# A message passing layer on one core: the edge stage with z in place in PSUM, and GpSimd left with the gathers

## The chip, the core and the metric

The kernel runs on one core of a Trainium2 chip. The core has TensorE (PE in the profile; its weight loads are PEld), VectorE (DVE), ScalarE (ACT), GpSimd (POOL) and SyncE (SP), and 16 DMA engines. The metric is device time in microseconds (us), from the kernel's start to its end; lower is better.

## The reference

One layer of a graph network over 1250 nodes and 20000 edges, in float32. The edges are sorted by their destination `dst`, and low node numbers have many more edges than high ones.

```
h      = relu(layernorm(x))                       # 1250 x 512
emb    = edge_attr @ W_edge + b_edge              # 20000 x 128 @ 128 x 512
msg    = relu(h[src] + emb)                       # 20000 x 512
aggr   = segment_sum(msg, dst, 1250)
h      = (1 + eps) * h + aggr
h      = gelu(layernorm(h @ W1 + b1))             # then W2, residual, layernorm
out    = x + layernorm(h + gelu(h @ M1) @ M2)
```

## The kernel before, in words

The kernel has three parts. First the node rows are normalized and written to DRAM as `gather_table` (with `b_edge` added), and DVE works out a plan from `dst`. Then comes the edge stage, of which this case is about. Last comes the node stage: W1, W2, M1 and M2, with layer norms between.

A **tile** is 128 edges, a **pair** two tiles, a **group** four tiles (`TPG`). There are 157 tiles with edges in 40 groups (`NG`); the last group has one such tile, and the kernel before computes two there. For each group:

- SP loads the transposed edge attributes into `attr_raw`. ACT rounds the first three tiles (`SPLIT`) to float32r, `attr_hi` (line 561). The rest, `attr_lo`, is subtracted by POOL for tiles 0 and 1 (line 455) and by DVE for tile 2 (line 922).
- PE multiplies by `W_edge` (`embed`). Tiles 0 to 2 take three float32r products each (lines 1100 to 1102), tile 3 one plain float32 product (line 1119), which the profile shows as two records. Pair 0 goes to `ps_u0` or `ps_t1` by turns, pair 1 to `ps_u1`.
- POOL gathers the source rows, one indirect DMA for a tile (line 472), by way of a small copy of the indices every two groups (`idx_now`, line 463). `rows` has two groups.
- DVE adds embedding and rows into `z` in SBUF (line 912, `z_done`). ACT writes `msg_hi`, relu of z rounded (line 660), and DVE writes `msg_lo`, the rest (line 916).
- ACT makes the 0/1 matrix `onehot` that says which node of a 128-node window each edge goes to: four squares into `apart` (line 594), then a relu (line 599).
- PE adds the messages into one PSUM half of `ps_t0` by `onehot` times `msg_lo` and `msg_hi` (line 1134, `scatter_last`).

Where the sorted edges pass from one window to the next inside a group (a **crossing**; there are nine), PE reads more of the plan into registers, adds the tiles of the old window with `onehot_first` (`scatter_extra`), and begins the new window with an identity product of the node rows (line 1127). ACT makes `onehot_first` (lines 606 and 613) and copies the old window out (line 624).

Each engine runs its own instructions in program order, and semaphores tie them together. There is no scheduler: the order is written out by hand in each engine's `group` or `step`. Most groups lie in loops whose body has four groups.

In the first four groups W1 is loaded, rounded by ACT (line 574) and its low part subtracted by DVE (line 939). The node stage does the same for later weights on POOL (line 504).

## Time and profile before

| | us |
|---|---|
| median of 3 runs (572.99 to 575.85) | 574.79 |
| the profiled execution, its own time | 573.92 |
| its span, first to last instruction | 572.0 |
| of it, first gather (27.4) to the last window copied out (311.7) | 284.3 |

Busy over the span: PE 468.2 (82%), DVE 410.2 (72%), POOL 337.1 (59%), ACT 307.4 (54%). The mean granted clock of TensorE is 0.966 of full speed. These shares mix the stages: in the edge stage the order of the engines is another, and a share says little there until the waits are read with it. "Idle before" is the time in which an engine did nothing ahead of an instruction, and the arrow names what ended it; "issue" means that the profile shows no wait.

### The profile page before, as it was taken

What the parts mean: (1) busy time and instruction counts of PE and PEld (TensorE: products, weight loads), DVE (VectorE), ACT (ScalarE), POOL (GpSimd) and SP (SyncE); (2) the same over time, 40 slices, a digit from 0 to 9 for tenths busy, and PEclk for the clock granted to TensorE, in tenths of its full rate; (3) what the DMA queues carried; (4) which work ended last, traced back from release to release, by engine and by line L of the source; (5) the groups of instructions that cost most, each with busy time, mean ns of one, the idle gap of its engine ahead of it and who ended that gap; (6) DMA issues with size and microseconds to landing.
All of it is one profiled execution on the core that took longest, in us unless ns stands there. A gap on an engine that the chain in (4) does not pass through costs nothing.

```text
span 572.0 us, 8417 instructions
## 1 busy us (share of the span) xinstructions
PE 468.2 (82%) x1959; PEld 356.2 (62%) x1960; DVE 410.2 (72%) x554; ACT 307.4 (54%) x569; POOL 337.1 (59%) x363
## 2 busy tenths in 40 slices
PE   1255887879777877889767999999999699999994
PEld 0133555656455554566545887778887489888883
DVE  7958869777767686779773577888999964473465
ACT  3848567676667685777872344446555556003100
POOL 4778878778787776778740244435777553150142
PEclk9999889899999999899997999999999799999998
DMA  8577666676666665676531922243441122021032
GB/s 279 215 243 246 207 202 205 187 204 184 199 194 196 197 202 167 187 211 206 166 111 42 328 75 73 92 146 112 147 147 56 55 74 74 19 93 37 5 106 73
DMA packets 34347, 85.27 MB, mean 149 GB/s; under 512 B 4928, under 2 KB 5264, under 8 KB 34320
## 3 DMA queue, kind: packets, MB, share of 16 engines
q0 software_dynamic: 12640, 41.43, 24.7%
q1 hardware_dynamic: 20864, 42.74, 22.4%
q10 hardware_dynamic: 816, 0.77, 0.5%
q8 instruction: 13, 0.21, 0.2%
q14 instruction: 14, 0.11, 0.1%
HBM read 72.34 MB, written 5.24 MB: 136 GB/s over the span
## 4 chain that ended last, share of the span: by engine, by line
PE 34%; issue 19%; DVE 18%; POOL 17%; DMA 6%; ACT 4%; POOLq 1%; DVEq 1%; another core or an unknown queue 0%; ACTq 0%; SPq 0%
POOL rows L472 11%; PE ps_t L1134 6%; DVE work L993 5%; PE ps_u L1100 5%; PE ps_u L1102 5%; PE ps_u L1101 5%; DMA rows<-gather_table,idx_now 4%; PE ps_t L1100 4%; PE ps_t L1101 4%; PE ps_t L1102 4%; DVE z L912 3%; POOL rstd L499 3%; POOL attr_lo L455 2%; ACT squares L716 2%; DVE lhs_lo L972 2%
## 5 line engine op out<-in xcount | busy, mean ns | idle before, releaser
L472 POOL DMA_INDIRECT rows<-gather_table,idx_now x158 | 173.1, 1095 | 57.4 <-issue 40.6
L912 DVE TENSOR_TENSOR z<-ps_u,rows 128x1024 f32<-128x1024 f32 x59 | 72.1, 1223 | 65.1 <-DMA rows<-gather_table,idx_now 32.7
L916 DVE SCALAR_TENSOR_TENSOR msg_lo<-z,msg_hi 128x1024 fp32r<-128x1024 f32 x79 | 96.2, 1258 | 0.0
L497 POOL TENSOR_TENSOR var_eps<-mv,eps_t 128x1 f32<-128x1 f32 x40 | 11.6, 290 | 143.3 <-ACT squares L716 77.1
L660 ACT ACTIVATE msg_hi<-z 128x1024 fp32r<-128x1024 f32 x79 | 82.4, 1043 | 2.3 <-DVE z L912 2.1
L1100 PE MATMUL ps_u<-we_hi,attr_lo 128*128 128x512 f32 x79 | 37.4, 474 | 45.6 <-POOL attr_lo L455 32.3
L1100 PE MATMUL ps_u<-w_hi,lhs_lo 128*128 128x512 f32 x160 | 64.7, 404 | 4.3 <-DVE lhs_lo L972 3.1
L1102 PE MATMUL ps_u<-w_hi,lhs_hi 128*128 128x512 f32 x160 | 62.9, 393 | 0.0
L1101 PE MATMUL ps_u<-w_lo,lhs_hi 128*128 128x512 f32 x160 | 62.8, 392 | 0.0
L1134 PE MATMUL ps_t<-msg_lo,onehot 128*128 128x512 f32 x146 | 62.1, 425 | 0.0
L1134 PE MATMUL ps_t<-msg_hi,onehot 128*128 128x512 f32 x146 | 60.4, 414 | 0.0
L1100 PEld LDWEIGHTS ps_u<-we_hi,attr_lo 128*128 128x128 f32 x79 | 15.8, 200 | 62.5 <-DVE z L912 19.6
L561 ACT ACTIVATE attr_hi<-attr_raw 128x384 fp32r<-128x384 f32 x40 | 20.6, 518 | 57.3 <-PE ps_u L1119 38.4
L594 ACT ACTIVATE apart<-iota,neg_rel_last 128x128 f32<-128x128 f32 x160 | 50.6, 387 | 0.0
L499 POOL TENSOR_TENSOR rstd<-var_eps,minus_half 128x1 f32<-128x1 f32 x40 | 40.3, 1007 | 3.1
L504 POOL TENSOR_TENSOR w_lo<-w_raw,w_hi 128x512 f32 (+1 forms) x24 | 35.0, 1462 | 9.4 <-ACT w_hi L711 9.4
L1119 PE MATMUL ps_u<-we_raw,attr_raw 128*128 128x512 f32 x78 | 40.5, 601 | 0.0
L1100 PE MATMUL ps_u<-ff_in_hi,w_lo 128*128 128x512 f32 (+1 forms) x96 | 34.8, 363 | 5.0 <-DVE ff_in_lo L968 5.0
L1100 PEld LDWEIGHTS ps_u<-w_hi,lhs_lo 128*128 128x128 f32 x160 | 30.1, 188 | 11.8 <-issue 3.3
L747 ACT ACTIVATE ff_full<-ps_u 128x512 f32<-128x512 f32 (+1 forms) x24 | 12.6, 527 | 43.4 <-PE ps_u L1102 39.5
L1134 PEld LDWEIGHTS ps_t<-msg_lo,onehot 128*128 128x128 f32 x146 | 30.2, 207 | 7.5 <-issue 0.5
L1101 PE MATMUL ps_u<-ff_in_lo,w_hi 128*128 128x512 f32 (+1 forms) x96 | 34.8, 362 | 0.0
(158 smaller groups left out, 1096.3 us busy)
## 6 DMA issues: line engine op xcount, KB each, us to landing
attr_raw<-in_attr_t SPq DMA_DIRECT2D x40, 256.0 KB
w_raw<-in_W SPq DMA_DIRECT2D x24, 256.0 KB, 2.7
tile_in<-mid SPq DMA_DIRECT2D x10, 512.0 KB, 3.2
res<-in_x SPq DMA_DIRECT2D x20, 256.0 KB, 2.6
xin<-in_x SPq DMA_DIRECT2D x5, 512.0 KB, 7.4
gather_table<-tab SPq DMA_DIRECT2D x5, 512.0 KB, 2.8
out<-work SPq DMA_DIRECT2D x10, 256.0 KB, 2.1
rows<-gather_table,idx_now POOLq DMA_INDIRECT x158
```

Source lines behind the costliest of these rows:

```text
L472: g.indirect_dma_start(rows[:, q, t, :], None, gather_table[:, :], bass.IndirectOffsetOnAxis(idx_now[:, slot, q * TPG + t:q * TPG + t + 1] ...
L499: g.tensor_tensor(rstd[:, slot:slot + 1], var_eps[:, slot:slot + 1], minus_half[:, 0:1], ALU.pow).then_inc(LN[ln]["rstd"], 1)
L504: g.tensor_tensor(w_lo[1 - s % 2][:, cols], w_raw[:, p, :], w_hi[1 - s % 2][:, cols].bitcast(f32), ALU.subtract).then_inc(w_lo_done, 1)
L594: last = a.activation(apart[:, e, :], iota[:, 0:P], ACT.Square, bias=neg_rel_last[:, ds(gr * TPG + e, 1)])
L660: a.activation(pair(msg_hi, r, p), pair(z, r % 2, p), ACT.Relu).then_inc(msg_hi_done, 1)
L912: v.tensor_tensor(pair(z, q, p), embedded(p, q)[:, :], rows[:, q, 2 * p:2 * p + 2, :].rearrange("p a d -> p (a d)"), ALU.add).then_inc(z_d ...
L916: v.scalar_tensor_tensor(pair(msg_lo, r, p), pair(z, r % 2, p), 0.0, pair(msg_hi, r, p).bitcast(f32), ALU.max, ALU.subtract).then_inc(msg_ ...
L1100: t.matmul(o, lhs[1][cols], rhs[0][rcols], start=first, stop=False)
L1101: t.matmul(o, lhs[0][cols], rhs[1][rcols], start=False, stop=False)
L1102: return t.matmul(o, lhs[0][cols], rhs[0][rcols], start=False, stop=last)
L1119: last = t.matmul(o, attr_raw[:, r, e * P:(e + 1) * P], we_raw[:, :], start=True, stop=True)
L1134: last = t.matmul(summed_in(bank), selection[:, e, :], m[:, r, e * D:(e + 1) * D], start=False, stop=(e == tiles[-1] and m is msg_hi), ski ...
```

## The change

- POOL only gathers in the edge stage, straight from `src_idx`; the 157 gathers are written out one after the other without a loop. `idx_now` and its copy are gone.
- `rows` has three groups instead of two. Each gather of a pair waits for the z of six pairs before (four before the change).
- z has no buffer of its own: DVE adds the rows in place in PSUM (`embedded`), over three pair buffers `ps_u0`, `ps_u1`, `ps_t1` in turn, and `msg_hi` and `msg_lo` read PSUM. PE may write a pair buffer again only when `msg_lo` of the pair three before is done; before, it waited for z.
- Two tiles of a group, the first of each pair, are split in three products, and the other two go through plain float32. DVE makes all of `attr_lo`. `attr_raw` has six slots, `msg_hi`, `msg_lo` and `onehot` have three groups.
- DVE's order alternates: add of a pair, then `msg_low` of the pair before it. ACT does `msg_hi` of pair 0 first, then `apart`, `msg_hi` of pair 1, `onehot`, and then the split of the group after next.
- PE scatters pair by pair, with an embedding ahead of each. The last group has one tile.
- W1 is loaded, rounded and split in the last groups. POOL makes its low parts after its last gather.
- Loop bodies have six groups; three groups stand ahead of the loop and seven behind.

```diff
-RING = 4
-HALF = EG // 2
-SPLIT = 3 * P
+RING = 3
+ATTRS = 6
+SPLIT = 2 * P
+HEAD, TAIL = 3, 7
...
-        attr_raw = sb("attr_raw", [P, RING, EG], f32, edge)
+        attr_raw = sb("attr_raw", [P, ATTRS, EG], f32, edge)
...
-        rows = sb("rows", [P, 2, TPG, D], f32, edge)
-        z = sb("z", [P, 2, 4 * D], f32, edge)
+        rows = sb("rows", [P, RING, TPG, D], f32, edge)
...
+        def embedded(g, p):
+            return (ps_u[0], ps_u[1], ps_t[1])[g.bank(p)][:, 0:D * g.in_pair(p)]
...
+            sp.wait_ge(emb_done[1], NG - TAIL + 1)
+            load_attr(NG - 1, (NG - 1) % ATTRS)
+            for c in range(W1_CHUNKS):
+                load_w1(c)
...
-            def two_groups(j, slot, split=True, pairs=2):
-                copy_idx(j, slot)
-                for q in range(2):
-                    gather(2 * j + q, q, 0, slot)
-                    if split:
-                        split_attr(2 * j + q, 2 * slot + q)
-                    if q == 0 or pairs == 2:
-                        gather(2 * j + q, q, 1, slot)
...
-            two_groups(0, 0, split=False)
-            with pool.Fori(0, NG // 4 - 1) as jj:
-                two_groups(2 * jj + 1, 1)
-                two_groups(2 * jj + 2, 0)
-            two_groups(NG // 2 - 1, 1, pairs=PAIRS)
+            for e in range(TILES):
+                group, pair_now = fixed(e // TPG), e % TPG // 2
+                if e % 2 == 0 and e // 2 >= 2 * RING:
+                    pool.wait_ge(z_done, e // 2 - 2 * RING + 1)
+                g.indirect_dma_start(rows[:, group.r, e % TPG, :], None, gather_table[:, :],
+                                     bass.IndirectOffsetOnAxis(src_idx[:, e:e + 1].bitcast(u32), 0)
+                                     ).then_inc(rows_in[group.slot(pair_now)], 16)
+            for c in range(W1_CHUNKS):
+                cols = slice(c * W1_COLS, (c + 1) * W1_COLS)
+                pool.wait_ge(w_hi_done, c + 1)
+                g.tensor_tensor(w_lo[0][:, cols], w1_raw[:, cols], w_hi[0][:, cols].bitcast(f32),
+                                ALU.subtract).then_inc(w_lo_done, 1)
...
-            def split_attr(gr, r):
-                q = r % 2
-                act.wait_ge(attr_in[r], 16 * (gr // RING + 1) if isinstance(gr, int) else 4 * (gr - r) + 16)
-                if not zero(gr, 1):
-                    act.wait_ge(emb_done[1], gr - 1)
-                a.activation(attr_hi[:, q, :], attr_raw[:, r, 0:SPLIT], ACT.Copy).then_inc(attr_hi_done, 1)
+            def split_attr(g):
+                act.wait_ge(attr_in[g.k], 16 * (g.attr_lap + 1))
+                if not zero(g.gr, 1):
+                    act.wait_ge(emb_done[1], g.gr - 1)
+                a.activation(by_pair(attr_hi[:, g.q, :]), apart_tiles(attr_raw[:, g.k, :]), ACT.Copy).then_inc(attr_hi_done, 1)
...
+            def message_high(g, p):
+                act.wait_ge(z_done, 2 * g.gr + p + 1)
+                if not zero(g.gr, RING - 1):
+                    act.wait_ge(scattered, g.gr - RING + 1)
+                a.activation(pair(msg_hi, g, p), embedded(g, p), ACT.Relu).then_inc(msg_hi_done, 1)
+            def group(g):
+                message_high(g, 0)
+                measure_last(g)
+                if g.pairs == 2:
+                    message_high(g, 1)
+                select_last(g)
+                if not (isinstance(g.gr, int) and g.gr >= NG - 2):
+                    split_attr(g.next(2))
+                events(g.gr, g.q)
...
+            for gr in range(NG - TAIL, NG):
+                group(fixed(gr))
+                c = gr - (NG - 1 - W1_CHUNKS)
+                if 0 <= c < W1_CHUNKS:
+                    w1_high(c)
...
+            def add_rows(g, p):
+                dve.wait_ge(rows_in[g.slot(p)], 32 * g.lap + 16 * g.in_pair(p))
+                dve.wait_ge(emb_done[p], g.gr + 1)
+                v.tensor_tensor(embedded(g, p), embedded(g, p),
+                                rows[:, g.r, 2 * p:2 * p + g.in_pair(p), :].rearrange("p a d -> p (a d)"), ALU.add).then_inc(z_done, 1)
+            def msg_low(g, p):
+                dve.wait_ge(msg_hi_done, 2 * g.gr + p + 1)
+                v.scalar_tensor_tensor(pair(msg_lo, g, p), embedded(g, p), 0.0, pair(msg_hi, g, p).bitcast(f32),
+                                       ALU.max, ALU.subtract).then_inc(msg_lo_done, 1)
+            def split_attr(g):
+                dve.wait_ge(attr_hi_done, g.gr + 1)
+                v.tensor_tensor(by_pair(attr_lo[:, g.q, :]), apart_tiles(attr_raw[:, g.k, :]), by_pair(attr_hi[:, g.q, :].bitcast(f32)),
+                                ALU.subtract).then_inc(attr_lo_done, 1)
+            def group(g):
+                add_rows(g, 0)
+                if not (isinstance(g.gr, int) and g.gr + 1 >= NG):
+                    split_attr(g.next(1))
+                if not zero(g.gr):
+                    msg_low(g.next(-1), 1)
+                if g.pairs == 2:
+                    add_rows(g, 1)
+                msg_low(g, 0)
+            split_attr(fixed(0))
...
+            def embed(g, p):
+                pe.wait_ge(attr_lo_done, g.gr + 1)
+                if not zero(2 * g.gr + p if isinstance(g.gr, int) else g.gr, 2):
+                    pe.wait_ge(msg_lo_done, 2 * g.gr + p - 2)
+                o = embedded(g, p)
+                if g.in_pair(p) == 2:
+                    t.matmul(o[:, D:2 * D], attr_raw[:, g.k, (2 * p + 1) * P:(2 * p + 2) * P], we_raw[:, :], start=True, stop=True)
+                three(o[:, 0:D], (attr_hi, attr_lo), (slice(None), g.q, slice(p * P, (p + 1) * P)),
+                      (we_hi, we_lo), (slice(None), slice(0, D)), True, True).then_inc(emb_done[p], 1)
...
+            def scatter_last(g, p, bank, touched):
+                if p == 0:
+                    pe.wait_ge(onehot_ready, g.gr + 1)
+                pe.wait_ge(msg_lo_done, 2 * g.gr + p + 1)
+                last = visit(onehot[g.r], g, bank, range(2 * p, 2 * p + g.in_pair(p)), g.tiles - 1, touched)
+                if p == g.pairs - 1:
+                    last.then_inc(scattered, 1)
+            def step(g):
+                before = None if zero(g.gr) else g.next(-1)
+                if before:
+                    event, bank, *touched = plan_part(ENG.PE, before.gr, EVENT, 1 + TPG, D)
+                for p in range(2):
+                    n = g.next(1 if p == 0 else 2)
+                    if not (isinstance(n.gr, int) and (n.gr >= NG or n.pairs < 2 - p)):
+                        embed(n, 1 - p)
+                    if before:
+                        if p == 0:
+                            scatter_extra(before, event)
+                        if p < before.pairs:
+                            scatter_last(before, p, half(bank), touched)
```


On DVE, in the loop of the kernel before, a group with pair 0 in `ps_u0` reads:

```order
L912 TENSOR_TENSOR z<-ps_u0,rows 128x1024 [waits emb_done0]
L921 REGISTER_ALU
L922 TENSOR_TENSOR attr_lo<-attr_raw,attr_hi 128x128 [waits attr_hi_done]
L910 REGISTER_ALU [waits rows_in01]
L912 TENSOR_TENSOR z<-ps_u1,rows 128x1024 [waits emb_done1,msg_lo_done]
L915 ISA
L916 SCALAR_TENSOR_TENSOR msg_lo<-z,msg_hi 128x1024 [waits msg_hi_done]
L915 REGISTER_ALU
L916 SCALAR_TENSOR_TENSOR msg_lo<-z,msg_hi 128x1024 [waits msg_hi_done]
```

In the change the same place in DVE's loop reads:

```order
L939 TENSOR_TENSOR ps_u0<-ps_u0,rows 128x1024 [waits emb_done0]
L949 REGISTER_ALU
L950 TENSOR_TENSOR attr_lo<-attr_raw,attr_hi 128x256 [waits attr_hi_done]
L943 ISA
L944 SCALAR_TENSOR_TENSOR msg_lo<-ps_t1,msg_hi 128x1024 [waits msg_hi_done]
L939 TENSOR_TENSOR ps_u1<-ps_u1,rows 128x1024 [waits emb_done1,rows_in1]
L943 ISA
L944 SCALAR_TENSOR_TENSOR msg_lo<-ps_u0,msg_hi 128x1024 [waits msg_hi_done]
```

The adds write where they read, the two `msg_lo` of the group before no longer stand together, and the second one is now that of the same group.

On POOL, in the loop before, half of what two groups issue is:

```order
L463 COPY idx_now<-src_idx 128x8
L464 REGISTER_ALU
L469 ISA [waits idx_copied]
L472 DMA rows<-gather_table,idx_now 128x512 [waits z_done]
L472 DMA rows<-gather_table,idx_now 128x512
L454 REGISTER_ALU
L455 TENSOR_TENSOR attr_lo<-attr_raw,attr_hi 128x256 [waits attr_hi_done]
L469 REGISTER_ALU
L472 DMA rows<-gather_table,idx_now 128x512 [waits z_done]
L472 DMA rows<-gather_table,idx_now 128x512
```

In the change POOL's edge stage begins so, and goes on so:

```order
L514 DMA rows<-gather_table,src_idx 128x512 [waits table_saved,idx_in]
L514 DMA rows<-gather_table,src_idx 128x512 x11
L514 DMA rows<-gather_table,src_idx 128x512 [waits z_done]
L514 DMA rows<-gather_table,src_idx 128x512
L514 DMA rows<-gather_table,src_idx 128x512 [waits z_done]
```

Twelve gathers go ahead of the first wait (eight before), and nothing stands between the gathers.

On PE, one step of the first groups before has, from pair 1 of the next group to the test for a crossing:

```order
L246 TENSOR_LOAD plan
L1100 MATMUL ps_u1<-we_hi,attr_lo 128x512 [waits z_done,attr_last_lo_done]
L1101 MATMUL ps_u1<-we_lo,attr_hi 128x512
L1102 MATMUL ps_u1<-we_hi,attr_hi 128x512
L1119 MATMUL ps_u1<-we_raw,attr_raw 128x512
L1148 COMPARE_AND_BRANCH
L246 TENSOR_LOAD plan x2
```

In the change, the second embedding of such a step (pair 0 of the group after next) and the scatter behind it read:

```order
L1127 MATMUL ps_t1<-we_raw,attr_raw 128x512 [waits msg_lo_done,attr_lo_done]
L1117 MATMUL ps_t1<-we_hi,attr_lo 128x512
L1118 MATMUL ps_t1<-we_lo,attr_hi 128x512
L1119 MATMUL ps_t1<-we_hi,attr_hi 128x512
L1150 COMPARE_AND_BRANCH [waits msg_lo_done]
L1143 ISA
L1143 MATMUL ps_t0<-msg_lo,onehot1 128x512
L1143 MATMUL ps_t0<-msg_hi,onehot1 128x512
```

The first product of an embedding now waits for `msg_lo_done` where it waited for `z_done`, and it is the float32 product.

## Rows read from the trace of the kernel before

**Rows 1.** Windows of the edge stage: busy us and (count) by engine, clock, DMA share, GB/s.

```profile
41.80:114.40 72.60, 56.64 (x192) 39.77 (x193) 58.38 (x58) 48.95 (x91) 58.05 (x57) 0.91 0.68 210
114.40:298.30 183.90, 148.87 (x551) 103.38 (x549) 135.49 (x135) 134.80 (x269) 140.54 (x147) 0.98 0.64 188
```

**Rows 2.** Groups of instructions by line, 100 to 280 us: busy, mean ns | idle before.

```profile
L472 POOL DMA_INDIRECT rows<-gather_table,idx_now x108 | 116.1, 1075 | 39.2 <-issue 27.5 <-POOL idx_now L463 6.7 <-DVE z L912 4.9
L916 DVE SCALAR_TENSOR_TENSOR msg_lo<-z,msg_hi 128x1024 fp32r<-128x1024 f32 x53 | 63.8, 1244 | 0.0
L660 ACT ACTIVATE msg_hi<-z 128x1024 fp32r<-128x1024 f32 x53 | 55.3, 1043 | 0.0
L912 DVE TENSOR_TENSOR z<-ps_u,rows 128x1024 f32<-128x1024 f32 x40 | 48.9, 1223 | 45.2 <-DMA rows<-gather_table,idx_now 22.3 <-PE ps_u L1119 11.9 <-PE ps_u L1102 6.8
...
L455 POOL TENSOR_TENSOR attr_lo<-attr_raw,attr_hi 128x256 fp32r<-128x256 f32 x27 | 20.3, 750 | 0.5
...
L561 ACT ACTIVATE attr_hi<-attr_raw 128x384 fp32r<-128x384 f32 x26 | 13.5, 519 | 33.7 <-PE ps_u L1119 25.1 <-issue 6.9 <-remote 1.7
```

**Rows 3.** Timeline of POOL around 151 us: start, us, engine, line, instruction.

```profile
150.55 0.95 POOL L472 DMA_INDIRECT rows<-gather_table,idx_now  x1 [0.31 <-issue]
151.52 0.74 POOL L455 TENSOR_TENSOR attr_lo<-attr_raw,attr_hi 128x256 fp32r<-128x256 f32 x1
152.41 1.77 POOL L472 DMA_INDIRECT rows<-gather_table,idx_now  x1 [0.16 <-issue]
```

**Rows 4.** Timeline of DVE at the same place.

```profile
148.18 1.22 DVE L912 TENSOR_TENSOR z<-ps_t,rows 128x1024 f32<-128x1024 f32 x1
149.31 0.28 DVE L922 TENSOR_TENSOR attr_lo<-attr_raw,attr_hi 128x128 fp32r<-128x128 f32 x1
...
151.97 2.51 DVE L916 SCALAR_TENSOR_TENSOR msg_lo<-z,msg_hi 128x1024 fp32r<-128x1024 f32 x2
```

**Rows 5.** Timeline of PE: the same place, then a float32 product.

```profile
152.38 0.49 PE L1100 MATMUL ps_u<-we_hi,attr_lo 128*128 128x512 f32 x1 [1.77 <-POOL attr_lo L455]
...
104.41 1.02 PE L1119 MATMUL ps_u<-we_raw,attr_raw 128*128 128x512 f32 x2
105.26 0.49 PE L1100 MATMUL ps_t<-we_hi,attr_lo 128*128 128x512 f32 x1
```

**Rows 6.** Chain that ended last, the piece at 160 us.

```profile
160.48 1.81 PE ps_t L1134 x8
```

**Rows 7.** Timeline of PE at a window crossing.

```profile
162.81 1.02 PE L1119 MATMUL ps_u<-we_raw,attr_raw 128*128 128x512 f32 x2
166.18 0.49 PE L1134 MATMUL ps_t<-msg_lo,onehot_first 128*128 128x512 f32 x1 [2.34 <-issue]
...
168.12 1.02 PE L1127 MATMUL ps_t<-acc,ident 128*128 x2
168.58 0.80 PE L1100 MATMUL ps_u<-we_hi,attr_lo 128*128 128x512 f32 x1
```

**Rows 8.** Timeline of ACT at a window crossing.

```profile
153.92 1.05 ACT L660 ACTIVATE msg_hi<-z 128x1024 fp32r<-128x1024 f32 x1
156.46 1.28 ACT L606 ACTIVATE apart_first<-iota,neg_rel_first 128x128 f32<-128x128 f32 x4 [1.49 <-issue]
157.87 0.63 ACT L613 ACTIVATE onehot_first<-apart_first 128x512 fp32r<-128x512 f32 x1
```

**Rows 9.** Source line L606: all its instructions.

```profile
L606 ACT ACTIVATE apart_first<-iota,neg_rel_first x36: 384/387/403, 122.9 to 292.3; 128x128 f32<-128x128 f32 x36
```

**Rows 10.** Timeline of DVE at the end of the edge stage.

```profile
298.32 1.22 DVE L912 TENSOR_TENSOR z<-ps_t,rows 128x1024 f32<-128x1024 f32 x1
...
311.05 0.69 DVE L959 COPY acc<-ps_t  x1 [8.11 <-PE ps_t L1134]
```

**Rows 11.** Timeline of PE: the first product of the node stage.

```profile
313.95 0.47 PE L1100 MATMUL ps_u<-w_hi,lhs_lo 128*128 128x512 f32 x1 [1.07 <-DVE lhs_lo L972]
```

**Rows 12.** Groups of the page: the POOL weight splits.

```profile
L504 POOL TENSOR_TENSOR w_lo<-w_raw,w_hi 128x512 f32 (+1 forms) x24 | 35.0, 1462 | 9.4 <-ACT w_hi L711 9.4
```

More of the change, by code:

```diff
@@ L3 @@
 from contextlib import ExitStack, nullcontext
+from dataclasses import dataclass
 P = 128
@@ new lines, in group @@
+            def group(g):
+                add_rows(g, 0)
+                if not (isinstance(g.gr, int) and g.gr + 1 >= NG):
+                    split_attr(g.next(1))
+                if not zero(g.gr):
+                    msg_low(g.next(-1), 1)
+                if g.pairs == 2:
+                    add_rows(g, 1)
+                msg_low(g, 0)
+            split_attr(fixed(0))
+            for gr in range(HEAD):
+                group(fixed(gr))
+            with dve.Fori(0, LOOPS) as j:
+                for k in range(ATTRS):
+                    group(looped(j, k))
@@ L955, in _ @@
+            for gr in range(NG - TAIL, NG):
+                group(fixed(gr))
             hi = window(plan_part(ENG.DVE, NG - 1, HI, 1, NT)[0])
```

271 lines of the change are left out of this document (93 added, 178 removed).

## Prediction

> **What bounds the kernel now.** I read the windows first, to part the edge stage from the rest and to get a rate that the page's shares can't give. The fourth add (pair 3, of pairs 0 to 78) begins at 41.8 us, pair 24 at 114.4 and the last pair at 298.3. So the 21 pairs ahead of the first crossing take 72.6 us, which is 6.91 us a group, and the 54 pairs (27 groups) after it 183.9 us, 6.81 a group [rows 1]. The nine crossings of the second part (36 squares, four each, from 122.9 us on) [rows 9] therefore cost nearly nothing now: something else sets the pace.
>
> The groups by line say what. In 180 us, 27 groups, POOL is busy 116.1 us with gathers and 20.3 with attribute splits, and is idle 39.2 ahead of gathers, mostly "issue", which is the 0.31 us that stands before each gather even with nothing to wait for [rows 2, 3]. With the index copies that is all of the 180 us. DVE in the same stretch is idle 45.2 us before its adds, and the largest releaser is the gather's DMA [rows 2]. POOL is the bound and DVE waits for what POOL issues late.
>
> The timelines show a second fault. A gather takes 0.95 us, but the one at 152.41 takes 1.77, and it starts while DVE runs its two `msg_lo` at 151.97, which take 2.51 [rows 3, 4]. The mean of 1.075 [rows 2] is made of such cases: counted over both timelines, 21 of 158 gathers take over 1.5 us, and all 21 start beside a DVE instruction with two SBUF inputs (`msg_lo`, or the W1 split); none of the 64 that start beside the add, which has one input in PSUM, does.
>
> **The change, by the floor of each engine for a group.** POOL: four gathers at 0.95 plus 0.31, 5.04 us; if they keep their mean of 1.075, 5.54 [rows 2, 3]. The splits, the index copies and the waits behind them go. A rule of the Trainium skill bears on this (SBUF — State Buffer, Who interferes with whom): a VectorE instruction with two SBUF inputs contends with a GpSimd instruction that reads SBUF, and one with at most one SBUF input does not. `msg_lo` now reads PSUM and `msg_hi`, so by that rule POOL has its 5.04, and the rival of costly gathers below would fall. The rows beside the add agree.
>
> DVE: an add lets the next instruction start 1.13 us later (148.18 to 149.31) [rows 4]. Two adds and two `msg_lo` make 4.55; a split of 256 columns instead of 128 (0.28 us [rows 4]) about 0.35, an estimate. Together 4.9; by full durations (1.223, 1.244, 0.42) it would be 5.35 [rows 2]. I know of no row in which DVE writes PSUM. From below, nothing, since the add already reads it; from above, another 1.22 if the write doubled it. The nearest rows are reads from PSUM (1.223) and `msg_lo` all in SBUF (1.244) [rows 2]: no dearer, so I take nothing.
>
> The other rule speaks against the change. The Trainium skill (VectorE: DVE Perf Modes, The TRN2 errata) gives a fixed cost of 120 cycles for a VectorE read from PSUM and 58 from SBUF. At 0.96 GHz that is an estimated 0.065 us on each `msg_lo`, 4.9 us over the stage, and would turn my 547 into 552. The rows above do not bear it out, so the sum goes without it.
>
> PE: eight scatter products take 1.81 us, 0.226 each [rows 6], and a float32 product 0.85 (104.41 to 105.26) [rows 5]. Before, 17 and one: 4.7. Now 14 and two: 4.87. ACT: busy 48.95 us over 10.5 groups, 4.66 each [rows 1], and slightly less with 256 columns in place of 384 (0.519 us now [rows 2]).
>
> So three engines stand at 4.9 to 5.04, and the waits between them decide. With three pair buffers, `msg_lo` of a pair releases the embedding of the third pair on. That takes 0.85 + 3 x 0.226 plus the tail of the last product and two handovers of about 0.12 (POOL's split ends at 152.26, PE starts at 152.38) [rows 3, 5], about 2.0 us. In that time DVE has one add and one `msg_lo` to do, 2.27, or 2.6 with the split. It fits with little to spare, so every slip is passed on. I take 5.2 us a group, between 5.04 and 5.54.
>
> **Crossings.** PE is idle 2.34 us while it reads the plan (163.83 to 166.18), begins the window in 0.46 (168.12 to 168.58) [rows 7] and does one more tile, 0.45 [rows 6]: 3.25 us. ACT loses 3.5 us (154.97 to 158.5) [rows 8] between the messages of two groups; what DVE still has to do (a split, a `msg_lo`, an add) covers about 1.7 of it. Until now POOL's slowness hid both: PE had two us a group to spare. Now nobody has. At least PE's 3.25 shows, at most 3.25 + 1.8 = 5.05; I take 4.2, nine times 37.8 us.
>
> **Ends.** At the start the first add must wait for a split on DVE and PE's three products behind it, while the first gather loses its index copy; the pair at 41.8 should stand about where it does, 2 us either way. The W1 splits leave the first groups of DVE, whose cost is inside the 72.6. At the end the last add to the copied window takes 12.7 us (298.32 to 311.05) [rows 10]. One tile instead of two in the last group, half an add and half a `msg_lo` less, and one `msg_lo` that goes ahead of the last add save about 3. POOL's four W1 parts of 1024 columns are at most 2 x 1.46 us each [rows 12], 11.7 in all. POOL is up to six pairs ahead, 15 us before the last add, and the first product needs them only 15.6 us after it (298.32 to 313.95) [rows 10, 11], less the 3. What hides them is that lead; without it they still end before. I cost them at nothing. ACT's four roundings fall among the last groups, up to 1 us each if not covered; DMA moves 210 GB/s now [rows 1] and would have to move 6.9/5.2 of it, 280, which the deeper buffers should bear.
>
> **Sum.** First part 10.5 x 5.2 = 54.6 for 72.6, saving 18.0. Second part 27 x 5.2 + 37.8 = 178.2 for 183.9, saving 5.7. End 3. Together 26.7 off the profiled 573.9, which is 0.9 below the median: 547.
>
> **Rivals.**
> - Crossings fully serial, at 5.05: 45.5 instead of 37.8, so 555. ACT's delay comes a pair or so ahead of PE's, which speaks for it; that ACT stands idle part of each group speaks against. Chance 0.2, the dearer PSUM read with it.
> - The gathers keep their mean, 5.54 a group: 37.5 x 0.34 = 12.8 more, so 560. For it: 280 GB/s of DMA, and SBUF work on DVE that stays (the split). Against: none of the 64 beside an add is long. 0.12.
> - Everything fits: 5.04 a group and 3.25 a crossing, 14.5 less, so 532. 0.17. Below 528 only if DVE's floor of 4.9 binds and crossings overlap with something: 0.06.
> - Slower: the add in place costs more than the add did. DVE sets the pace, so x us on each add adds 75x. The gain of 26.7 is gone at x = 0.36, and 0.6, half of the doubling, gives 592. Nothing in the rows speaks for it but that no row shows it. 0.06.
> - The change does not do what it says: the pair buffers, held until `msg_lo` instead of z, return so late that the freed POOL only waits. From 5.9 us a group the stage takes what it took, so 574. The loop over three pairs is then the bound, 8.85 us, against the 6.9 that I add up (2.0, four instructions of DVE at 1.13 and a split of 0.35). 0.04.
> - My forecast, 541 to 552: 0.35.
>
> **Range.** From 530 (all fits, with the start 2 us better) to 566 (5.54 a group with crossings at 4.9 or so): it leaves out 0.06 below and about 0.12 above. A measurement here can tell about 0.5%, 2.9 us, from no change. Faster holds all cases but the two of lost gain: 0.90; within 0.5%: 0.04; slower: 0.06.
>
> **What the profile after would show.** POOL's gathers all near 0.95 with none beside `msg_lo` stretched, and POOL ahead, so that its idle time ends with z. Adds that wait for PE or for nothing, no longer for the rows' DMA. Before the first crossing 5.2 us a group; at each crossing one gap of DVE before `msg_lo` (ACT) and one before an add (PE), 4 us together. Adds in place of 1.22 us. W1's parts on POOL ended before the first product. It would be wrong if the adds or `msg_lo` in PSUM are longer, if PE waits for `msg_lo` outside crossings, or if the first product waits for W1.

## The result and the profile after

The changed kernel took 594.0 us (593.0 to 595.5) beside 575.3 (573.0 to 576.6) for the kernel before on the same chip: ratio 1.033, 95% interval 1.029 to 1.038. It is slower, where 547 was forecast. The experiments below show that this number depends on something outside the kernel: the same kernel, unaltered, took 562.8 in another session (ratio 0.976, interval 0.970 to 0.981), then 592.5 and 594.0 in two more. The kernel before took 575.2 to 577.0 in all of them. Ratios compare fast runs alone; one run of `h1_after_third` in the table below, 596.9, was a slow one.

From the page of the changed kernel, profiled where it took 594 (groups by line: busy us, mean ns, then the idle time before them and its releaser; last, a line of the DMA issues):

```profile
span 593.1 us, 7864 instructions
PE 484.5 (82%) x1915; PEld 354.3 (60%) x1916; DVE 401.0 (68%) x550; ACT 298.3 (50%) x569; POOL 284.7 (48%) x306
...
L514 POOL DMA_INDIRECT rows<-gather_table,src_idx x157 | 149.0, 949 | 128.9 <-DVE ps_u L939 65.3
L939 DVE TENSOR_TENSOR ps_u<-ps_u,rows 128x1024 f32<-128x1024 f32 (+1 forms) x53 | 64.6, 1218 | 70.1 <-PE ps_u L1119 34.9
...
L944 DVE SCALAR_TENSOR_TENSOR msg_lo<-ps_u,msg_hi 128x1024 fp32r<-128x1024 f32 (+1 forms) x53 | 64.0, 1208 | 5.1 <-issue 4.3
...
rows<-gather_table,src_idx POOLq DMA_INDIRECT x157
```

Every duration came out as forecast: gathers 0.949 us (they were 1.075, [rows 2]), the add in place 1.218, `msg_lo` from PSUM 1.208. GpSimd now waits for z. W1 costs nothing: GpSimd's last part of it ends at 322.6, the first product that needs it starts at 334.3. And yet DVE is idle 70 us before the adds of this line (85 before all 79). Its timeline, at three of them:

```profile
46.69 1.23 DVE L939 TENSOR_TENSOR ps_u<-ps_u,rows 128x1024 f32<-128x1024 f32 x1 [4.82 <-remote]
...
55.83 1.23 DVE L939 TENSOR_TENSOR ps_u<-ps_u,rows 128x1024 f32<-128x1024 f32 x1 [6.79 <-remote]
...
120.19 1.23 DVE L939 TENSOR_TENSOR ps_u<-ps_u,rows 128x1024 f32<-128x1024 f32 x1 [3.32 <-remote]
```

These are pairs 3, 4 and 24. Ten adds wait so, 33.5 us in all. "Remote" names no cause; it stands where the increment that ended the wait is on record, but no instruction that makes it had ended shortly before. TensorE's timeline ahead of the third, and then SyncE's behind it, say more:

```profile
116.36 0.40 PE L1119 MATMUL ps_u<-we_hi,attr_hi 128*128 128x512 f32 x1
...
118.83 0.39 PE L1119 MATMUL ps_u<-we_hi,attr_hi 128*128 128x512 f32 x1
...
119.75 0.39 PE L1143 MATMUL ps_t<-msg_hi,onehot 128*128 128x512 f32 x1
122.94 1.45 PE L1127 MATMUL ps_t<-we_raw,attr_raw 128*128 128x512 f32 x2 [2.81 <-DVE msg_lo L944]
```
```profile
120.39 0.33 SPq L384 DMA_DIRECT2D attr_raw<-in_attr_t  x1
```

Pair 24's embedding ends at 116.76, pair 25's at 119.22. DVE waits for the semaphore increment of the first and passes at 120.13; ACT, waiting for the scatter that ended at 117.68, passes at 120.18; SyncE, waiting for the second, issues at 120.39. In the trace's list of semaphore updates these three increments of TensorE stand at 120.10, 120.16 and 120.23. The work was done in time; its completions were reported up to 3.3 us late, in one burst. I call this a late completion. Those that hold adds further on are mostly 3.1 to 3.6 us late, and at the start they are worse: the embedding of pair 4 ends at 43.81 and is reported at 55.74.

The page's DMA line gives the second clue: it has no time to landing, because the trace holds only 989 of the 2512 semaphore increments of the gathers. The rest were lost from the recording, as were increments of the engines (of the 79 embeddings, 54 are on record). The time between the adds of pairs 3, 24 and 78 ([rows 1] for before), in the two sessions (`g1_after_again` is the kernel of the 563 us):

| | before | forecast | after, 594 us | g1_after_again |
|---|---|---|---|---|
| add of pair 3 at | 41.8 | 41.8 | 46.7 | 41.8 |
| pair 3 to 24 | 72.6 | 54.6 | 73.5 | 54.3 |
| pair 24 to 78 | 183.9 | 178.2 | 197.8 | 191.4 |
| pair 78 to the first product | 15.6 | 12.6 | 16.3 | 16.3 |
| increments of gathers on record | 1631 of 2528 | | 989 of 2512 | 2512 of 2512 |

### The profile page after: what moved, and what is told of

It reads as the page before. It is cut to its first block, busy times and chain, and to the rows that moved or that the text cites. A ratio compares the mean times of both kernels' runs of the same rounds, so it can differ in the third digit from the quotient of the medians.

```text
span 593.1 us, 7864 instructions
## 1 busy us (share of the span) xinstructions
PE 484.5 (82%) x1915; PEld 354.3 (60%) x1916; DVE 401.0 (68%) x550; ACT 298.3 (50%) x569; POOL 284.7 (48%) x306
## 4 chain that ended last, share of the span: by engine, by line
PE 43%; DVE 26%; issue 15%; ACT 6%; another core or an unknown queue 5%; POOL 3%; DMA 1%; DVEq 1%; ACTq 0%; POOLq 0%
PE ps_t L1143 9%; DVE msg_lo L944 6%; DVE work L1010 5%; PE ps_u L1117 5%; PE ps_u L1118 5%; PE ps_u L1119 5%; PE ps_u L1127 4%; PE ps_t L1119 4%; PE ps_t L1117 4%; PE ps_t L1118 4%; DVE ps_u L939 3%; PE ps_t L1127 3%; POOL rstd L527 2%; PE ps_t L1136 2%
## 5 line engine op out<-in xcount | busy, mean ns | idle before, releaser
L514 POOL DMA_INDIRECT rows<-gather_table,src_idx x157 | 149.0, 949 | 128.9 <-DVE ps_u L939 65.3
L939 DVE TENSOR_TENSOR ps_u<-ps_u,rows 128x1024 f32<-128x1024 f32 (+1 forms) x53 | 64.6, 1218 | 70.1 <-PE ps_u L1119 34.9
L1127 PE MATMUL ps_u<-we_raw,attr_raw 128*128 128x512 f32 x104 | 58.6, 646 | 41.9 <-DVE attr_lo L950 24.1
L690 ACT ACTIVATE msg_hi<-ps_u 128x1024 fp32r<-128x1024 f32 (+1 forms) x53 | 53.7, 1013 | 68.9 <-DVE ps_u L939 56.9
L944 DVE SCALAR_TENSOR_TENSOR msg_lo<-ps_u,msg_hi 128x1024 fp32r<-128x1024 f32 (+1 forms) x53 | 64.0, 1208 | 5.1 <-issue 4.3
L1127 PEld LDWEIGHTS ps_u<-we_raw,attr_raw 128*128 128x128 f32 x104 | 20.5, 207 | 53.8 <-issue 42.4
L1117 PE MATMUL ps_u<-we_hi,attr_lo 128*128 128x512 f32 x53 | 44.0, 830 | 0.0
L939 DVE TENSOR_TENSOR ps_t<-ps_t,rows 128x1024 f32<-128x1024 f32 x26 | 31.9, 1227 | 15.6 <-PE ps_t L1119 13.5
L1127 PE MATMUL ps_t<-we_raw,attr_raw 128*128 128x512 f32 x52 | 31.0, 680 | 12.3 <-issue 6.1
L532 POOL TENSOR_TENSOR w_lo<-w_raw,w_hi 128x512 f32 (+1 forms) x24 | 34.9, 1456 | 8.0 <-ACT w_hi L743 8.0
L1117 PEld LDWEIGHTS ps_u<-w_hi,lhs_lo 128*128 128x128 f32 x160 | 30.1, 188 | 11.9 <-issue 3.3
L1143 PE MATMUL ps_t<-msg_lo,onehot_first 128*128 128x512 f32 x21 | 12.3, 587 | 29.3 <-issue 29.3
```

The source lines that it names most:

```text
L514: g.indirect_dma_start(rows[:, group.r, e % TPG, :], None, gather_table[:, :], bass.IndirectOffsetOnAxis(src_idx[:, e:e + 1].bitcast(u32), ...
L532: g.tensor_tensor(w_lo[1 - s % 2][:, cols], w_raw[:, p, :], w_hi[1 - s % 2][:, cols].bitcast(f32), ALU.subtract).then_inc(w_lo_done, 1)
L690: a.activation(pair(msg_hi, g, p), embedded(g, p), ACT.Relu).then_inc(msg_hi_done, 1)
L939: v.tensor_tensor(embedded(g, p), embedded(g, p), rows[:, g.r, 2 * p:2 * p + g.in_pair(p), :].rearrange("p a d -> p (a d)"), ALU.add).then ...
L944: v.scalar_tensor_tensor(pair(msg_lo, g, p), embedded(g, p), 0.0, pair(msg_hi, g, p).bitcast(f32), ALU.max, ALU.subtract).then_inc(msg_lo_ ...
L1117: t.matmul(o, lhs[1][cols], rhs[0][rcols], start=first, stop=False)
```

## The experiments

Each kernel is one edit to the changed kernel, timed beside the kernel before; kernels of one letter shared a chip. Every run, timed or not, comes with its span and clock and so was recorded; nothing here shows what a kernel takes unrecorded.

| kernel | us | ratio to before, interval | increments on record |
|---|---|---|---|
| e1_z_sbuf | 565.7 | 0.981, 0.976 to 0.987 | 1267 |
| e2_ahead3 | 584.3 | 1.016, 1.010 to 1.022 | 1034 |
| e3_scatter_whole | 596.4 | 1.036, 1.030 to 1.042 | 1078 |
| e4_extra_later | 605.3 | 1.051, 1.045 to 1.056 | 1062 |
| f1_z_sbuf_ahead3 | 560.9 | 0.975, 0.968 to 0.981 | 2511 |
| f2_plan_early | 573.4 | 0.996, 0.994 to 0.999 | 2512 |
| f3_no_branch | 565.6 | 0.984, 0.976 to 0.992 | 2512 |
| f4_sp_incs | 565.6 | 0.981, 0.972 to 0.989 | 2512 |
| g1_after_again | 562.8 | 0.976, 0.970 to 0.981 | 2512 |
| g2_sp_incs_again | 564.0 | 0.978, 0.973 to 0.984 | 2512 |
| g3_no_branch_one_read | 567.5 | 0.983, 0.976 to 0.989 | 2512 |
| g4_z_sbuf_all | 557.3 | 0.965, 0.959 to 0.971 | 2512 |
| h1_after_third | 592.5 | 1.022, 1.016 to 1.029 | 1040 |
| h2_sp_incs_double | 610.8 | 1.060, 1.056 to 1.065 | 1077 |
| h3_z_sbuf_all_again | 561.6 | 0.973, 0.969 to 0.976 | 1392 |
| i1_after_fourth | 594.0 | 1.036, 1.029 to 1.042 | 989 |
| i2_pool_slow | 582.5 | 1.014, 1.009 to 1.019 | 2045 |
| i3_z_sbuf_ahead4 | 562.9 | 0.980, 0.976 to 0.984 | 1112 |

The sessions e, h and i have lossy recordings, f and g complete ones. The first session's is lossy as well. f and i ran on the same chip, so it is not the chip.

**e1_z_sbuf.**

```diff
-                v.tensor_tensor(embedded(g, p), embedded(g, p),
+                v.tensor_tensor(summed(g, p), embedded(g, p),      # z[:, g.q, ...] in SBUF; ACT and msg_low read it
...
-                    pe.wait_ge(msg_lo_done, 2 * g.gr + p - 2)
+                    pe.wait_ge(z_done, 2 * g.gr + p - 2)
```

> One part undone: the sum z goes to a buffer in SBUF again (four pairs of it), TensorE waits for the add and no longer for msg_lo before it overwrites a pair of PSUM, and ACT and VectorE read z from SBUF. All else is the changed kernel's. Theory A (the loss comes from holding a PSUM pair until msg_lo, which leaves TensorE no lead, so that each crossing and each late release of an add shows in full): TensorE gets its lead back, a crossing costs about 2 us in place of 5.8 and the ten stalls of adds of about 3.3 us shrink, while gathers beside msg_lo are stretched again (mean 1.08 us), which sets 5.5 us a group; total about 550 us, well below both. Rival B (the loss comes from gathers that run up to six pairs ahead, or from the start): this kernel keeps that lead, so it keeps the stalls of adds and takes 580 us or more. Rival C (three pair buffers and PSUM have no part in it): no change from 594.

566, not 550, but 28 below the changed kernel in the same kind of session. Most stalls of adds are gone. Left are the start (11 us for pairs 3 and 4), one of 10.6 us and four of 1.8 to 3.5 us (pairs 65 to 68, 9.9 us together). The gathers are stretched again, as theory A says, and further than its 1.08 us:

```profile
L519 POOL DMA_INDIRECT rows<-gather_table,src_idx x157 | 189.6, 1208 | 62.9 <-issue 45.1
```

949 ns with `msg_lo` reading PSUM, 1208 with it reading two SBUF tiles; the edit leaves GpSimd's own instructions as they are.

**e2_ahead3.**

```diff
-                if e % 2 == 0 and e // 2 >= 2 * RING:
-                    pool.wait_ge(z_done, e // 2 - 2 * RING + 1)
+                if e % 2 == 0 and e // 2 >= 3:
+                    pool.wait_ge(z_done, e // 2 - 2)
```

> The changed kernel, but GpSimd waits before the gathers of pair n for the add of pair n-3 and no longer of pair n-6, so that at most three pairs of gathers are under way. Theory A (TensorE has no lead, its own completions come late): the stalls of adds, in which the embedding had ended over 3 us before, stay in number and length, and the time stays within 1% of 594. Rival B (too many gathers in flight delay the semaphores): the ten stalls, 33.5 us together, go, and the time falls to about 565.

Between the two: the adds of pairs 3 and 4 no longer wait (pair 4 at 45.2 instead of 55.8), which is all of its 10 us; later late completions stay, 29.5 us in twelve adds. In a lossy session, six pairs of gathers in flight cost the start, where 12 gathers coincide with the first embeddings, and little behind it. In the complete one they cost nothing there: g1, which has them, starts at 41.8.

**e3_scatter_whole and e4_extra_later.**

```diff
-                        if p < before.pairs:
-                            scatter_last(before, p, half(bank), touched)
+                if before:
+                    for p in range(before.pairs):
+                        scatter_last(before, p, half(bank), touched)
```

e4 moves `scatter_extra(before, event)` to stand directly ahead of this loop as well.

> One part undone: the scatter of a group's two pairs is issued whole behind the second embedding of the step, as before the change, in place of one pair behind each embedding. Theory A: the second embedding of a step starts 0.9 us earlier at a crossing, the next one later; the loop over three pair buffers is tighter or the same: within 1% of 594. Rival D (the interleaving of scatter and embedding is what makes adds wait, and keeps TensorE without a gap): the stalls change, and the time falls below 585.

> As e3_scatter_whole, and the extra work of a crossing (plan reads, start of the new window, first selection) stands behind the second embedding of the step and no longer ahead of it. Theory A: TensorE has about 1.8 us of work more to give VectorE before the crossing's 5 us begin, so each of nine crossings costs up to 1.8 us less than in e3_scatter_whole: up to 16 us faster than that one. Rival E (the crossing is paid on ACT, which delays the messages, or TensorE's lead can't grow since the buffers are held until msg_lo): no difference between the two beyond 0.5%.

e3 takes what the changed kernel takes in its lossy sessions (592 to 594), within 1%: the order of the scatter plays little part. e4 should have been up to 16 us faster than e3 and is 9 slower. The delay is not shortened by standing later in the step; it then falls on the next embedding.

**f1 to f4.** f1 is e1 and e2 together. The others:

```diff
 f2_plan_early
-                    event, bank, *touched = plan_part(ENG.PE, before.gr, EVENT, 1 + TPG, D)
+                    event, bank, *late = plan_part(ENG.PE, before.gr, EVENT, ANY, NG * NT + 1)
+                    touched, late = late[:TPG - 1], late[TPG - 1:]      # scatter_extra takes its cells from late
 f3_no_branch
-                            scatter_last(before, p, half(bank), touched)
+                            scatter_last(before, p, half(bank), None)
 f4_sp_incs
                     load_attr(g.gr + ATTRS, g.k)
+                    for _ in range(24):
+                        alone(sp)
```

> e1_z_sbuf and e2_ahead3 together: z in SBUF, and at most three pairs of gathers under way. In e1_z_sbuf the adds of pairs 3 and 4 still waited 11 us together, and one add waited 10.6; in e2_ahead3 the first two waits were gone. If the lead of the gathers is what the start pays for, whatever the rest does, the fifth add begins near 45 us instead of 56, and the time falls by about 10 us against e1_z_sbuf, to 555. If the two do not add up (GpSimd, with gathers of 1.2 us, needs the lead), it stays at 565 or rises.

> The changed kernel, but TensorE's queue reads all 18 plan cells of a group in one load at the head of the step, ahead of the embedding, and at a crossing it reads none. In the trace of the changed kernel the load at a crossing takes 1.70 us (at 305.46) and lies in TensorE's gap of 2.92. If the crossings are lost on TensorE's own queue, nine to twelve of them become about 1.7 us shorter each: 15 to 20 us less, about 577. If ACT's detour sets the crossing, the gap only changes its cause: 590 to 594.

> The changed kernel, but every tile's products for the last window are issued without a test whether the tile touches it (where it does not, they add zeros), which takes three branches and about six register instructions a group from TensorE's queue. If the late completions of TensorE (embeddings that had ended 3.3 us before the add was released, after TensorE had run 13 to 16 us without a gap) come from how much its queue has to do, they get fewer and the time falls by 10 us or more; if they come from the uninterrupted run alone, they stay, and the time is within 1% of 594, a few us being paid for the idle products at crossings.

> The changed kernel, but SyncE, which has nothing else to do, increments a semaphore that nobody waits for 24 times in each of the 30 groups of the loop. If completions of TensorE are late because the semaphore events of all engines and transfers together are too many, the late ones get more or longer: the time rises by 10 us or more. If it is a matter of TensorE and of its own queue, nothing changes: within 1% of 594.

f1 has its fifth add at 45.8, as expected, and takes 561, but e1 has no run in a session of this kind to set beside it. f4 was meant to make things worse and took 28 us less than the changed kernel had. An edit that only adds work to an idle engine can't do that, so the comparison with 594 was at fault, and with it those of f1 to f3. None of the four traces has a late completion, and all four recordings are complete (f1 lacks one increment). Here theories A to D fell as the cause of the whole 594.

**g1 to g4**, one session, the changed kernel among them. g3 is f3 with the two reads of a crossing in one:

```diff
-                    lo, _, count, changed, bank_lo_now, bank_next = plan_part(ENG.PE, g.gr, LO, 6, max(NT, D))
-                    run, _, third, crossing, *touched = plan_part(ENG.PE, g.gr, RUN, 3 + TPG, NG * NT + 1)
+                    lo, _, count, changed, bank_lo_now, bank_next, run, _, third, crossing, *touched = plan_part(
+                        ENG.PE, g.gr, LO, ANY - LO, NG * NT + 1)
```

g4 is z in SBUF (e1), gathers four pairs ahead, no branches (f3) and the one read.

> The changed kernel itself, unaltered, beside two of the experiments on one chip. The first set of experiments (e1 to e4) and the changed kernel all showed late completions of TensorE, the second set (f1 to f4), taken on another chip, showed none at all, even in f4_sp_incs, which alters nothing on the working engines. If the late completions belong to the kernel, it takes 594 again with about ten adds held back. If they belong to the chip that it ran on, it takes what f4_sp_incs takes, about 566, where that one takes 566.

> f4_sp_incs again (24 increments a group on SyncE), now beside the changed kernel. If its 28 us are the kernel's, it takes about 566 and g1_after_again 594. If the chip decides, both take the same within 1%, 566 or 594.

> f3_no_branch, and the plan cells of a crossing are read by TensorE's queue in one load of 13 instead of two of 6 and 7. In the trace of f3_no_branch these two take 1.47 and 1.70 us, one behind the other, and the gap of TensorE (237.85 to 240.59) ends 1.5 us behind the second. If TensorE's queue sets the price of a crossing, nine to twelve of them get about 1.3 us shorter each, 12 to 15 us in all: 553 if late completions are absent. If ACT or VectorE set it, no change from 565.

> f1_z_sbuf_ahead3 with four pairs of gathers under way in place of three, no test of the tiles and one plan read. z in SBUF gives TensorE its lead back, so a crossing costs 2 us in place of 6, but gathers take 1.2 us in place of 0.95, and GpSimd then sets 6.0 us a group: 39 x 6.0 and the start give about 550. If the crossing's price is now small in g3_no_branch_one_read too, that one is level with it or faster.

g1 and g2 take the same, 563 and 564. The page of g1:

```profile
PE 473.4 (84%) x1915; PEld 347.6 (62%) x1916; DVE 401.1 (71%) x550; ACT 297.5 (53%) x569; POOL 283.8 (50%) x306
...
L939 DVE TENSOR_TENSOR ps_u<-ps_u,rows 128x1024 f32<-128x1024 f32 (+1 forms) x53 | 64.5, 1216 | 37.2 <-PE ps_u L1119 35.5
...
rows<-gather_table,src_idx POOLq DMA_INDIRECT x157, 4.0
```

The same busy times as in the first profile, half the idle time before the adds, no "remote", and the gathers have a time to landing. g3 is not faster than g1 but 5 us slower. Its one read of 13 cells takes 3.11 us where the reads of 6 and 7 take 1.47 and 1.70: the price is 0.24 us a cell, not one a read. f2, which reads all 18 cells in every group, pays for it: every second group takes 8.8 us, and it is some 10 us slower than g1. The f3 and g3 kernels issue idle products for tiles that a window does not touch, and gain nothing from the missing branches.

**h1 to h3**, to tie the lost records to the late completions. h2 is f4 with 48 increments, h3 is g4.

> The changed kernel unaltered, on a chip not chosen by us. It took 594 with about ten adds held back where it was first run, and 563 with none in g1_after_again. In the first trace only 989 of the 2512 semaphore increments of its gathers are on record, in the second all 2512. Theory F (where the recording of events loses events, TensorE's completions also come late, and a kernel that issues more events in the same time pays more): either all increments are on record and it takes 560 to 566, or about half are missing and it takes 590 to 597. Rival G (the two go their own ways): one without the other, or a time between.

> The changed kernel with 48 increments a group on SyncE that nobody waits for. Theory F: where h1_after_third has its increments all on record, no change within 1%; where they are missing, more completions are late and it takes 10 us or more longer than h1_after_third. Rival G: no change in either place.

> g4_z_sbuf_all again. It was the fastest, 557, where nothing was late. With z in SBUF TensorE has a lead that hides a late completion, as in e1_z_sbuf, which took 566 where e2 to e4 had late ones: 555 to 560 if nothing is late here, 560 to 570 if completions are late, in both cases below the kernel before.

The recordings of h are lossy, and both times are as theory F says; the reason that it gives for h2 is not what the trace shows. DVE's waits in h1 (engine, what it waited for: us in all, times, longest):

```profile
DVE ps_u L939 <- PE ps_u L1119: 34.5, 9, 5.5
DVE ps_u L939 <- remote: 28.3, 9, 7.4
...
DVE ps_t L939 <- remote: 6.5, 3, 3.1
```

The "remote" is back, 34.8 us. With 48 increments a group that nobody waits for the kernel takes 18 us more (593 to 611). In the complete session 24 of them cost nothing (562.8 and 564.0); 48 were not run there. These 18 us are no further late completions of TensorE: "remote" before the adds of h2 is 34.7 us, as in h1. What is new is SyncE's queue. Of its 1456 increments in h2, 75 take about 0.70 us, where none in f4 and g2 takes over 0.02, and the attribute loads behind them are issued late (that of group 17 at 144.4, in h1 at 115.1). ACT then waits for them, which it does not in h1:

```profile
ACT attr_hi L590 <- DMA attr_raw<-in_attr_t: 13.7, 7, 5.0
```

h3 takes 562 against 557 in the complete session.

**i1 to i3.** i2 behind every other gather, on spare tiles, leaving the result as it is:

```diff
+                if e % 2 == 0:
+                    g.tensor_tensor(spare[:, 2, :], spare[:, 0, :], spare[:, 1, :], ALU.subtract).then_inc(spare_set, 1)
+                    pool.wait_ge(spare_set, e // 2 + 2)
```

i3 is e1 with gathers four pairs ahead.

> The changed kernel unaltered once more, as the measure for the two beside it. With all 2512 semaphore increments of the gathers on record it takes 560 to 566, with about half of them missing 590 to 597 (so it was in all three runs so far).

> The changed kernel, but GpSimd subtracts two spare tiles of 128x256 in SBUF, which nobody waits for, behind every other gather, so that it needs about 6.7 us a group, as before the change, in place of 5.04. z stays in PSUM. In the changed kernel nine crossings cost about 6.5 us each, before the change 0.6. Theory A (a PSUM pair is held until msg_lo, so TensorE cannot run ahead and a crossing shows whatever else is slow): groups of 6.7 us and a crossing still at 3 us or more, total 585 to 600. Rival H (a crossing was hidden only because GpSimd was slow; slack alone covers it, wherever z lies): groups of 6.7 us, crossings at about nothing, total 570 to 578, as before the change.

> z in SBUF and four pairs of gathers under way, with the tests of the tiles and the two plan reads of the changed kernel (g4_z_sbuf_all had neither). The reads take 0.24 us a cell, whether in one load or in two (1.47 and 1.70 against 3.11), so that the one load saved nothing; the products without a test cost 0.45 us for each tile that the window does not touch. If that is the whole difference, this one is level with g4_z_sbuf_all or 2 to 5 us faster: 553 to 560 where nothing is late, 558 to 565 where completions are.

i1: lossy, 594, as expected. i2 slows GpSimd to 6.46 us a group (adds of pairs 3 and 24 at 45.16 and 112.95), which also thins out the events: 2045 increments are on record, and the stalls of 3.3 us are gone. It misses both expectations, 582 against 585 to 600 (A) and 570 to 578 (H). Its adds of pairs 24 to 78 lie 192.5 us apart (112.95 to 305.42), where g1 has 191.4: behind the first part, slowing GpSimd cost about nothing. DVE's wait at a crossing, 5.81 us, is the one that g1 shows in the next section:

```profile
249.27 1.23 DVE L945 TENSOR_TENSOR ps_t<-ps_t,rows 128x1024 f32<-128x1024 f32 x1 [5.81 <-PE ps_t L1125]
```

i3 takes 563, level with h3.

## Why the prediction was wrong

**What held.** The floors and the pace between crossings. Gathers are not stretched beside `msg_lo` (rival "the gathers keep their mean" is out; e1 restores the stretch). The prediction counts 64 gathers that start beside an add; between an add's start and end I find 47, none of them long, so its reading stands. The add in place costs nothing extra, so the rival at 592 is out although the number is close. Most groups away from crossings take 4.87 to 4.95 us where 5.2 was taken. With a complete recording pairs 3 to 24 take 54.3 us, forecast 54.6, and the start stands at 41.8. W1 is hidden.

**Step one that failed: a step that is missing.** The sum has no term for a completion that is reported late. Where the recording loses events there are ten such waits, 33.5 us, about the whole of the 594 less 563. That they go with the lossy recording is shown: four profiles of the changed kernel, 989, 1040, 989 and 2512 increments on record, 594, 592, 594 and 563 us; both kinds on one chip; and no embedding reported over 0.3 us late in the eight complete traces. The engines' queues are held back too. In ten of the eleven lossy traces (not in i2's) some register or semaphore instructions take about 0.70 us where their like take 0.04 to 0.2: ten on TensorE's queue between 124 and 137 us of e1, where its add waited 10.6 us, and the 75 of SyncE in h2. In the eight complete traces none in the edge stage, the plan reads aside, takes over 0.45. That the recording holds the engines back, and how, is argued from this; a third thing that both loses records and delays engines is not excluded. The Trainium skill (NOTIFIC — the notification-queue block, Overflow: three behaviours, one of which stalls the engine) says that the block's inner pipeline holds its producers back rather than lose a record; the late completions and the 0.70 us instructions fit that, the lost semaphore records do not, and no run here reads the block's counters.

Why does the kernel before not suffer, with 897 of its 2528 increments missing? In seven of the ten cases TensorE had run 13 to 16 us without a gap, and before the change it never ran over 12: a gap of 1.5 to 3 us stood every one or two groups, shorter ones between. That a gap lets the reports catch up is argued, not shown; the start (pairs 3 and 4, TensorE mostly idle) doesn't fit; what helps there is fewer gathers ahead (e2). In the trace of before only one embedding on record is reported over 1 us late (pair 65, 2.1 us; its add waited 1.5), so late completions hardly occurred there, though records were lost. A lead of TensorE covers them too: the kernel with z in SBUF goes from 557 to 562 between sessions (g4, h3), the changed one from 563 to 594. So the change opened the kernel to a disturbance whose sign, lost records, was there before. The page of before showed it: its line for `rows` has no landing time either, and I did not read that as a warning.

**Step two: the crossings**, taken at 4.2, "at least PE's 3.25". In the complete recording nine of them take 191.4 - 27 x 4.94 = 58.0 us, 6.4 each, which is 20 us more than the 37.8 of the sum. TensorE at one of them in g1, then DVE:

```profile
220.80 0.40 PE L1119 MATMUL ps_u<-we_hi,attr_hi 128*128 128x512 f32 x1
224.82 0.49 PE L1143 MATMUL ps_t<-msg_lo,onehot_first 128*128 128x512 f32 x1 [3.62 <-DVE msg_lo L944]
225.15 0.40 PE L1143 MATMUL ps_t<-msg_hi,onehot_first 128*128 128x512 f32 x1
225.38 1.07 PE L1136 MATMUL ps_t<-acc,ident 128*128 x2
225.84 1.04 PE L1143 MATMUL ps_t<-msg_lo,onehot 128*128 128x512 f32 x1
226.68 0.63 PE L1143 MATMUL ps_t<-msg_hi,onehot 128*128 128x512 f32 x1
...
227.96 1.85 PE L1127 MATMUL ps_t<-we_raw,attr_raw 128*128 128x512 f32 x2
...
230.12 0.40 PE L1119 MATMUL ps_t<-we_hi,attr_hi 128*128 128x512 f32 x1
```
```profile
223.60 1.22 DVE L944 SCALAR_TENSOR_TENSOR msg_lo<-ps_u,msg_hi 128x1024 fp32r<-128x1024 f32 x1
230.63 1.23 DVE L939 TENSOR_TENSOR ps_t<-ps_t,rows 128x1024 f32<-128x1024 f32 x1 [5.81 <-PE ps_t L1119]
```

The gap is 3.62 us, not 2.34 [rows 7]: in the trace of TensorE's queue the two reads take 1.47 us from 219.61 and 1.70 from 221.24, and 1.8 us of branches and register instructions follow until 224.8. (The row names `msg_lo`, which happened to end at 224.82; the queue had passed its wait for it at 223.1.) Here one tile belongs to the first window; begin and scatter of the last window follow. Behind the gap the clock falls, as the windows of TensorE show (busy us, granted clock, DMA share, GB/s):

```profile
221.20:224.80 3.60, 0.00 (x0) 1.00 0.64 209
224.80:227.00 2.20, 2.18 (x6) 0.82 0.63 171
227.00:229.90 2.90, 2.90 (x7) 0.55 0.32 88
229.90:232.00 2.10, 2.10 (x10) 1.00 0.00 0
```

For 2.9 us TensorE runs at about its lower level, 1.2 GHz, and most of the embedding that DVE waits for is in it. Over ten us around seven crossings of g1 the clock is 0.83, 0.83, 0.83, 0.83, 1.00, 0.66 and 1.00; the two crossing groups at 1.00 take 9.3 and 9.5 us, those at 0.83 11.1 to 11.4, the one at 0.66 12.6 (an eighth, ahead of pair 30, has 3.4 us at the lower level and takes 11.0). By this comparison of few groups the clock is worth about 1.8 us in five of seven; the windows above agree (2.9 x 0.45 + 2.2 x 0.18 = 1.7). It was no term of mine. ACT's detour shows as well, ahead of it: the group before the crossing takes 5.8 to 7.4 us, mostly 6.2. Gap, clock and ACT are serial. The rival "crossings fully serial, 5.05" is nearest in kind, and short by this.

What exposes them, holding z in PSUM or GpSimd's new speed, i2 and g4 tell apart. With z in PSUM and GpSimd at near its old pace (i2), seven adds behind pair 24 wait 4.2 to 5.8 us for TensorE, the same part takes 192.5 us, and the gaps of TensorE are as long as in g1 (3.63 us where g1 has 3.62). No late completion is in its trace. The sum over GpSimd's pace, 192.5 - 27 x 6.46 = 18.1 or 2.0 a crossing, looks small only because GpSimd is up to six pairs ahead and the groups between crossings run faster than 6.46. With z in SBUF and 5.9 us a group (g4: adds at 42.54, 104.49 and 281.19, so 176.7 - 27 x 5.9 = 17.4) a crossing costs 1.9, and no add behind pair 24 waits over 3.1 us for TensorE; g4's other edits gained nothing in f3 and g3. So it is holding z in PSUM, which leaves TensorE no lead, and "Until now POOL's slowness hid both" in the prediction was wrong: in the kernel before, which shows no cost [rows 1], z in SBUF was needed for that. DVE around a crossing in g4, where the longest wait is now ACT's:

```profile
213.60 0.43 DVE L957 TENSOR_TENSOR attr_lo<-attr_raw,attr_hi 128x256 fp32r<-128x256 f32 x1 [0.46 <-ACT attr_hi L593]
...
217.89 1.23 DVE L951 SCALAR_TENSOR_TENSOR msg_lo<-z,msg_hi 128x1024 fp32r<-128x1024 f32 x1 [1.59 <-ACT msg_hi L695]
219.03 1.22 DVE L946 TENSOR_TENSOR z<-ps_u,rows 128x1024 f32<-128x1024 f32 x1
220.83 0.43 DVE L957 TENSOR_TENSOR attr_lo<-attr_raw,attr_hi 128x256 fp32r<-128x256 f32 x1 [0.58 <-ACT attr_hi L593]
```

**Step three: the end**, forecast 3 us shorter, is 0.7 longer (287.47 to 303.79). The halved last add and `msg_lo` are there, 0.69 us each, but the path runs through TensorE's last crossing, a gap of 4.76 us, to which they do not belong.

**The account.** With a complete recording: 547.2, less 7.0 for the faster groups, 20.2 more for the crossings, 3.7 for the end, less 0.3 for the first part, gives 563.8; the profiled g1 took 564.0. With the lossy one another 31 us. Of 594 - 547, two thirds are the missing step and one third the crossings and the end.

**A version that beats both.** g4 and h3, one kernel, take 557.3 and 561.6, ratios 0.965 and 0.973: the only kind here, with e1, f1 and i3, that was measured faster than before in both kinds of session. It gives back the unstretched gathers (1231 ns) and keeps the rest.

## What to carry over

Before you explain a wait without a named cause, see whether the events are all on record (a DMA line without a landing time says that they are not), and measure the changed kernel itself beside its variants, or you compare sessions. When a change takes away one engine's lead over another, price what that lead covered as a whole chain, the clock behind a gap included.

## What the hardware showed

- In sessions whose recordings lose events TensorE's completions are reported late, in bursts: about 3 us in the changed kernel, up to 11.9 at its start, 10.8 and 11.1 in e1 (pairs 30 and 31). Queue instructions there take 0.70 us now and then. The same chip has both kinds of session.
- Reading plan cells into registers costs TensorE's queue 0.24 us a cell (6: 1.47, 7: 1.70, 13: 3.11).
- Gathers on GpSimd take 0.949 us while VectorE reads one input from PSUM in `msg_lo`, 1.20 to 1.23 on average when both inputs lie in SBUF. The add in place in PSUM takes 1.22, no more than from PSUM to SBUF.
